# The output projection in chunks of 128 tokens, in the order of the output

## The reference

```python
# _gn: group norm, 32 groups of 12 channels, mean and variance over an image
x = x + attention(_gn(x), w_qkv, pos_emb, w_out, b_out)
# attention: shift 3 rows up and 3 columns left, windows of 7x7
qkv  = roll(x, (-3, -3)) @ w_qkv.T
dots = einsum('bhwid,bhwjd->bhwij', q, k) * 32 ** -0.5 + pos_bias + shift_mask
out  = einsum('bhwij,bhwjd->bhwid', softmax(dots), v)      # back to (B, H, W, 384)
out  = roll(out @ w_out.T + b_out, (3, 3))
```

## Time and profile before

| | us |
|---|---|
| runs | 4302.73, 4302.84, 4304.71; median 4302.84 |
| profiled execution | 4301.36 |
| its span | 4299.6 |

### The profile page before, as it was taken

How to read it: one execution, slowest core, us unless ns; L and a number is a source line. 1 busy time by engine, 2 the same in 40 slices (tenths; PEclk the granted TensorE clock), 3 DMA queues, 4 the chain that set the end, 5 groups by cost and what they waited for, 6 DMA issues and landing times.

```text
span 4299.6 us, 166334 instructions
## 1 busy us (share of the span) xinstructions
PE 4151.4 (97%) x65384; PEld 2982.5 (69%) x65384; DVE 3717.4 (86%) x9283; ACT 2271.7 (53%) x4225; POOL 2223.2 (52%) x1933
## 2 busy tenths in 40 slices
PE   3999999999999999999999999999999999999998
PEld 1677767777777767777677677777777777776776
DVE  5888888888888888888888888888888888888887
ACT  0555555555555555555555555555555555555554
POOL 1555555555555555555455555555555555555554
PEclk9999999999999999999999999999999999999999
DMA  4445444444444444444444444444534444444442
GB/s 125 102 111 126 106 112 117 110 114 112 113 118 106 115 120 103 113 125 106 112 116 112 113 113 111 120 110 108 123 101 113 125 105 112 117 111 113 102 105 62
DMA packets 231108, 479.07 MB, mean 111 GB/s; under 512 B 39009, under 2 KB 140898, under 8 KB 222818
## 3 DMA queue, kind: packets, MB, share of 16 engines
q1 hardware_dynamic: 230338, 468.43, 43.1%
HBM read 159.99 MB, written 77.07 MB: 55 GB/s over the span
## 4 chain that ended last, share of the span: by engine, by line
PE 65%; SPq 12%; DVE 10%; DMA 6%; ACT 4%; issue 4%; POOL 0%; DVEq 0%; ACTq 0%; POOLq 0%
PE ps_pj L1102 22%; PE ps_post L1198 12%; PE ps_pj L1098 9%; SPq L466 8%; DMA stack<-qk 6%; PE ps_post L1189 4%; PE ps_sa L1136 3%; PE ps_st L1166 3%; PE ps_pv L1182 3%; PE ps_pv L1181 2%; PE ps_pv L1180 2%; PE ps_st L1136 2%; ACT ph L681 2%; PE ps_pj L1086 2%; SPq L401 2%
## 5 line engine op out<-in xcount | busy, mean ns | idle before, releaser
L575 POOL TENSOR_TENSOR rb<-tq,cst 128x588 bf16<-128x588 bf16 x512 | 606.4, 1184 | 1698.7 <-ACT tq L668 1698.7
L607 ACT ACTIVATE qk<-ps_pj 128x392 f16<-128x392 f32 x768 | 381.9, 497 | 953.9 <-PE ps_pj L1102 947.8
L681 ACT ACTIVATE ph<-ps_st,sc 64x588 f16<-64x588 f32 x1024 | 772.2, 754 | 6.5
L1102 PE MATMUL ps_pj<-xh,wh 128*128 128x392 f16 x2304 | 765.9, 332 | 6.9 <-POOL xl L539 4.1
L1102 PE MATMUL ps_pj<-xh,wl 128*128 128x392 f16 x2304 | 765.0, 332 | 0.0
L1102 PE MATMUL ps_pj<-xl,wh 128*128 128x392 f16 x2304 | 764.8, 332 | 0.0
L878 DVE TENSOR_TENSOR qk<-ps_pj,qk 128x392 f16<-128x392 f32 x768 | 433.1, 564 | 383.7 <-ACT qk L607 377.6
L561 POOL TENSOR_TENSOR pl<-pf,ph 64x588 f16<-64x588 f32 x512 | 650.3, 1270 | 149.6 <-POOL rb L575 133.7
L547 POOL TENSOR_TENSOR xb<-xs,bout 98x384 f32<-98x384 f32 x512 | 513.8, 1004 | 107.9 <-DMA out<-xb 85.6
L966 DVE TENSOR_TENSOR pl<-pf,ph 64x588 f16<-64x588 f32 x512 | 529.0, 1033 | 0.1
L1180 PE MATMUL ps_pv<-vh,ph 128*128 128x33 f16 x6144 | 516.3, 177 | 1.6 <-DVE pl L966 1.6
(11 more groups left out here) (107 smaller groups left out, 8887.3 us busy)
## 6 DMA issues: line engine op xcount, KB each, us to landing
stack<-qk SPq DMA_DIRECT2D x1536, 147.0 KB
sx<-in_x SPq DMA_DIRECT2D x66, 1176.0 KB
xs<-in_x SPq DMA_DIRECT2D x384, 84.0 KB
out<-xb SPq DMA_DIRECT2D x384, 84.0 KB
xs<-in_x SPq DMA_DIRECT2D x384, 63.0 KB
out<-xb SPq DMA_DIRECT2D x384, 63.0 KB
xs<-in_x SPq DMA_DIRECT2D x128, 66.0 KB
out<-xb SPq DMA_DIRECT2D x128, 66.0 KB
```

The costliest lines, as they stand in the source:

```text
L575: nc.gpsimd.tensor_tensor(rb[:, :, :, :], tq[:, :, :].unsqueeze(2).broadcast_to([128, 2, HH, N]), const_of("own_head").unsqueeze(1).unsque ...
L681: e = nc.scalar.activation(ph[rows, :, w * PAD:w * PAD + N].rearrange("p (a h) n -> p a h n", a=2), ps_st[rows, :, 0:HH * N].rearrange("p ...
L1102: m = mm(ps_pj[bank][:, 0:RT].rearrange("p (w n) -> p w n", w=NW), wa[:, c, o:o + 128], xa[:, b, c, :, 0:N], **on)
```

## The change

The projection no longer takes the 98 tokens of a pair, but 128 tokens of a row in the order of the output. A row of 392 tokens gives three chunks of 128 and a rest of 8; the rests of 16 rows (two images) make one further chunk. `ath` and `atl` hold two whole rows, and ScalarE and VectorE write a pair's tokens into their places in the row (pair 3 in two parts, as it wraps). At p=3 ScalarE copies the rest of the last finished row to `overh` and `overl` (`keep_over`). The projection stands at the same place of a step, but at p=2, p=3 and p=0 for the chunks 0, 1 and 2 (`chunk_at`), and at p=1 only for the chunk of rests, in one row of 16. 392 projections of nine matmuls take the place of 512.

`xb` gets x by a second load from memory, directly in the order of chunks, six steps ahead (`load_chunk`); POOL adds the bias to it in place, two steps ahead. Stores are one DMA a chunk (two where an image ends within it or for the chunk of rests). The reload of `xs` no longer waits for the residual. In SP's program the stack is issued at p=1, after the store and chunk load of that step and before its reload. The new tiles take the place in memory of the raw weights.

```diff
+CHUNKS, OVER, SHARE = RT // 128, RT % 128, 128 // (RT % 128)
+XB, XB_AHEAD, BIAS_AHEAD = 8, 6, 2
+def chunk_at(t):
+    row, p = divmod(t, PAIRS)
+    row, part = {2: (row - 1, 0), 3: (row - 1, 1), 0: (row - 2, 2), 1: (row - 2, CHUNKS)}[p]
+    if not 0 <= row < ROWS or part == CHUNKS and row % SHARE != SHARE - 1:
+        return None
+    return row, part
...
+        ath = sb("ath", [128, 2, KC, RT], f16)
+        atl = sb("atl", [128, 2, KC, RT], f16)
+        overh = sb("overh", [128, KC, 128], f16)
+        overl = sb("overl", [128, KC, 128], f16)
...
+        def attended_parts(at, row, p):
+            to = at[:, row % 2, :, :].rearrange("p c (r w) -> p c r w", w=W)
+            from_ = at_out[:, :, 0:PT].rearrange("p c (r w) -> p c r w", w=2 * WS)
+            first = 2 * WS * p + DISP
+            n = min(2 * WS, W - first)
+            parts = [(to[:, :, :, first:first + n], from_[:, :, :, 0:n])]
+            if n < 2 * WS:
+                parts.append((to[:, :, :, 0:2 * WS - n], from_[:, :, :, n:2 * WS]))
+            return parts
...
-                reach(s_xb, 8 * tk.n + j + 1)
...
-                    if p == 2 and not (tk.last and odd):
-                        stack_row(1 - odd, unit_count(tk, 4 * odd + 1, "k", 2), 8 * n + 4 * odd)
...
-                    if not (tk.first and k < 3):
-                        store(t - 3, tk, k - 3)
+                    store(t)
+                    load_chunk(t + XB_AHEAD)
+                    if p == 1 and not (tk.last and odd):
+                        stack_row(1 - odd, unit_count(tk, 4 * odd + 1, "k", 2), 8 * n + 4 * odd)
...
+            def residual(t):
+                if not chunk_at(t):
+                    return
+                o = chunks_before(t)
+                pool.wait_ge(s_dense[o % XB], moved(o))
+                nc.gpsimd.tensor_tensor(xb[:, o % XB, :], xb[:, o % XB, :], bout[:, :], ALU.add).then_inc(s_xb, 1)
...
+                    if k % 4 == 3 and t > 3:
+                        keep_over(t - 4)
...
+            def keep_over(t):
+                row = t // PAIRS
+                act.wait_ge(s_al, t + 1)
+                if row >= SHARE:
+                    act.wait_ge(s_out, CHUNK_INDEX[row // SHARE * SHARE - 1, CHUNKS] + 1)
+                for over, of in ((overh, ath), (overl, atl)):
+                    ins = nc.scalar.activation(over[:, :, over_columns(row)], of[:, row % 2, :, RT - OVER:RT], ACT.Copy)
+                ins.then_inc(s_over, 1)
...
             def project_out(t):
-                pe.wait_ge(s_al, t + 1)
+                if not chunk_at(t):
+                    return
+                row, part = chunk_at(t)
+                pe.wait_ge(s_al, min(t - 2, PAIRS * ROWS))
+                need(pe, s_fin, chunks_before(t))
+                if part == CHUNKS:
+                    pe.wait_ge(s_over, row + 1)
                 for c in range(KC):
...
+                    if part == CHUNKS:
+                        high, low = overh[:, c, :], overl[:, c, :]
+                    else:
+                        high, low = (a[:, row % 2, c, part * 128:part * 128 + 128] for a in (ath, atl))
+                    for n_, (a, w) in enumerate(((high, woh), (high, wol), (low, woh))):
+                        m = mm(ps_post[:, 0:C], a, w[:, c, :], start=c == 0 and n_ == 0, stop=c == KC - 1 and n_ == 2)
```

More of the change, by code:

```diff
@@ L65, in constants @@
                 pin[place(kind, r, wc), kind, w * N + r * WS + c] = 1
[L66 to L69, removed]
+                pout[w * PAD + r * WS + c, place(0, r, wc)] = 1
+    pads = [w * PAD + i for w in range(2) for i in range(N, PAD)]
+    for n, p in enumerate(pads):
+        pout[p, PT + n] = 1
     tok = np.arange(N)
@@ L174, in ahead_image, with chunks_before, pieces, moved @@
         return self.image + (self.part + 1) // PARTS
+CHUNKS, OVER, SHARE = RT // 128, RT % 128, 128 // (RT % 128)
+IN_IMAGE = H // WS
+XB, XB_AHEAD, BIAS_AHEAD = 8, 6, 2
+STEPS = PAIRS * ROWS + 6
+def chunk_at(t):
[4 more added lines that the diff above has]
+    return row, part
+CHUNK_STEPS = [t for t in range(STEPS) if chunk_at(t)]
+CHUNK_INDEX = {chunk_at(t): o for o, t in enumerate(CHUNK_STEPS)}
+def chunks_before(t):
+    return sum(u < t for u in CHUNK_STEPS)
+def pieces(row, part):
+    if part == CHUNKS:
+        half = OVER * IN_IMAGE
+        return [(half * i, half * i + half, row // IN_IMAGE + i + 1 - SHARE // IN_IMAGE, None) for i in range(SHARE // IN_IMAGE)]
+    image, r = divmod(row, IN_IMAGE)
+    out, top, a, b = [], (WS * r + DISP) * W, part * 128, part * 128 + 128
+    cut = H * W - top
+    if a < cut:
+        out.append((0, min(b, cut) - a, image, top + a))
+    if b > cut:
+        out.append((max(a, cut) - a, 128, image, max(a, cut) - cut))
+    return out
+def moved(o):
+    return 16 * sum(len(pieces(*chunk_at(CHUNK_STEPS[i]))) for i in range(o % XB, o + 1, XB))
 def step_units(tk, k):
@@ L398, in move_row, with chunk_of, over_columns @@
             for a, b, d in pieces:
[L399 to L403, removed]
+                eng.dma_start(tile_of[a:b], d).then_inc(sems, 16)
+        x_flat, y_flat = (a.rearrange("b h w c -> b (h w) c") for a in (x, y))
+        def chunk_of(dram, image, token, n):
+            if token is None:
+                top = (WS * IN_IMAGE + DISP - 1) % H
+                return dram[image, top:H:WS, W - OVER:W, :]
+            return (x_flat if dram is x else y_flat)[image, token:token + n, :]
+        def attended_parts(at, row, p):
[7 more added lines that the diff above has]
+            return parts
+        def over_columns(row):
+            image, r = divmod(row, IN_IMAGE)
+            at = OVER * (IN_IMAGE * (image % (SHARE // IN_IMAGE)) + (r + 1) % IN_IMAGE)
+            return slice(at, at + OVER)
         def rows_of(tk, odd):
@@ L513, in _ @@
                 image(m)
[L514 to L517, removed]
+            for t in range(8 * (LAST + 1), STEPS):
+                store(t)
+                load_chunk(t + XB_AHEAD)
+            for o in range(len(CHUNK_STEPS) - XB, len(CHUNK_STEPS)):
+                sp.wait_ge(s_store[o % XB], moved(o))
         @block.gpsimd
@@ L583, in step @@
                         x_lows(tk, k)
-                    if not (tk.last and k + LEAD >= 8):
-                        residual(t + LEAD, n, k + LEAD)
+                    residual(t + BIAS_AHEAD)
             def image(m):
@@ L594, in _ @@
             split_probabilities(8 * (LAST + 1) - 1, 8 * (LAST + 1))
+            pool.wait_ge(s_pl[1], 8 * (LAST + 1))
+            for t in range(8 * (LAST + 1), STEPS):
+                residual(t + BIAS_AHEAD)
         @block.scalar
@@ L698, in _ @@
             attended_high(end - 1)
+            keep_over(end - 1)
         @block.vector
@@ L1012, in step @@
                     between(5)
-                    if not (tk.first and k < 3):
-                        output(t - 3, k - 3)
+                    output(t)
                     between(5)
@@ L1032, in _ @@
             normalize(end - 2)
-            output(end - 3, 5)
+            output(end)
             split_probabilities(end - 1)
@@ L1037, in _ @@
             normalize(end - 1)
-            output(end - 2, 6)
+            output(end + 1)
             attended_low(end - 1)
-            output(end - 1, 7)
+            for t in range(end + 2, STEPS):
+                output(t)
         @block.tensor
@@ L1219, in step @@
                         units(tk, k, 1)
-                    if not (tk.first and k < 3):
-                        project_out(t - 3)
+                    project_out(t)
                     if not (tk.last and k >= 4):
```

116 lines of the change are left out of this document (64 added, 52 removed).

## The result

| | before | changed |
|---|---|---|
| runs, us | 4302.73 to 4309.22 | 4250.67 to 4252.28 |
| median, us | 4303.77 | 4251.65 |
| ratio to before | | 0.9878, interval 0.9864 to 0.9892 |
| profiled execution / span, us | 4301.36 / 4299.6 | 4250.67 / 4248.9 |

The account below looks back on a forecast made before the run. TensorE, busy 97% of the span, was taken as the bound. Terms -29 - 7 - 17 + 4 - 1.5 + 4 = -47 us gave 4255 profiled, 4256 median; own range 4240 to 4270, wider range 4225 to 4290.

Parts of the forecast that it names:

- Projection at p=1: At p=1, k2 must wait for q2's low part, so removing 1.46 us of projection gains 0.28: 104 x 0.28 = 29 us.
- Finishing steps: p=1 steps where VectorE finishes the statistics: the output leaves its queue, 0.45 us gained in each of 15, 7 us.
- Stack: Issued one place earlier in SP's program, it starts 1.7 us earlier; 39 waits of first scores go, 17 us.
- Second load of x: 0.6 MB more to read in a row, 3.1 us of DMA time, costed at nothing.
- Rival 3: The second load of x delays the stack, so next row's first scores come 1.4 us late: 4449; chance 0.07.
- Strided writes: Runs of 14 columns make VectorE's low part 7% slower, paid at p=3: 4 us lost, bounds 0 and 59.
- Ends: Start: one dense projection gone, -1.5 us. End: four chunks behind the last pair where one stood, +4 us.
- Rival 4: A new TensorE wait of 1.2 us in each row could cost clock, 162 us: 4418; chance 0.02.

Follow-up runs that it names:

- e3: Changed kernel with nine, or six, matmuls of 384 columns put back at p=1, results unused, no output or store: nine 4279.75 us, six 4251.09 us.
- e4: Changed kernel with unit q2 moved right behind k1, ahead of the weighted values of p=1: 4163.43 us.
- e5: Changed kernel with chunk 2 projected at p=1 and the chunk of rests at p=0: 4205.0 us.
- e1: Kernel before with only the stack's place changed, issued at p=1 after that step's store and not at p=2: 4283.93 us.
- e2: Changed kernel with the stack issued at p=2 again, first thing of the step: 4254.61 us.
- e6: Changed kernel with each dense chunk of x loaded twice, the second time to a tile that nothing reads: 4249.71 us.
- e8: The e4 kernel with six matmuls added at p=1, results unused: 4252.25 us.
- e7: Kernel before with only unit q2 moved right behind k1 at p=1: 4282.19 us.

## Why the prediction was right, point by point

- *Projection at p=1*, forecast 104 x 0.28 = 29 us. The median step fell from 9.18 to 8.90, and the waits are 104. The wait's own length was forecast as 1.18 us between matmul starts, and the profile puts 1.01 us of idle time there, since x0's last matmul record ends 0.50 us behind the first one's start, where in the earlier trace rows the projection started at 0.34. e3 and e4 show the cause from both sides: work put into the wait is free, and the wait removed is time. The changed kernel has the counterproof in itself. In its last tick no x unit stands at p=1, so k2 uses the bank of k1, two units back, and not that of q2. There the step fell from 8.49 to 7.03 us, the whole 1.46, and the chain shows q2 and k2 (18 matmuls) without a gap:

```profile
4178.02 0.06 PE ps_sa L1257 x2
4178.07 3.06 PE ps_pj L1205 x18
4181.14 0.37 PE ps_st L1269 x4
```

  So the forecast's 104 steps were 102 that gained 0.28 to 0.29, this one, and one that lost: t=5, in the second row, takes 9.56 us after 9.18. There TensorE waits 0.97 us ahead of k2 and 0.50 for the shift rows, which the forecast had not looked at. Together they are 30 us. That the list also counts 104 waits is chance: they are the 102, the step t=5, and the kernel's first p=1 step, which had the wait before too.
- *Finishing steps*, 15 x 0.45 = 7 us. They fell from 11.28 to 10.87 us (the same distances), 15 x 0.41 = 6 us. That it is VectorE's lost output which gives this, as forecast, fits two runs: nine matmuls on TensorE leave these steps at 10.87 (e3), and with an output at p=1 they take 11.28 (e5).
- *Stack*, 17 us. The waits fell from 17.4 us to none. The amount is right, the reason given was half of it. I laid it to the new place in SP's program. e1 shows that the place alone does it in the kernel before; e2 shows that the changed kernel needs the new place for only 3.4 of the 17.4 us; by SP's queue the missing store of p=1 does the rest. The two overlap, and only one of them pays.
- *Second load of x*, nothing. e6: a third load is free too. Rival 3 falls.
- *Strided writes*, 7%, 4 us. VectorE's low part of a whole pair went from 456 to 472 ns, 3.5%; ScalarE's high part from 416 to 448, 8%; the copies of the rests take 212 ns, as estimated:

```profile
L1019 DVE TENSOR_TENSOR atl<-ps_post,ath 128x294 f16<-128x294 f32 x384 | 181.3, 472 | 2.7 <-ACT ath L747 1.6 <-issue 1.1
L747 ACT ACTIVATE ath<-ps_post 128x294 f16<-128x294 f32 x384 | 171.9, 448 | 10.6 <-PE ps_post L1292 2.0
...
L756 ACT ACTIVATE overh<-ath 128x24 f16<-128x24 f16 x128 | 27.2, 212 | 0.6 <-DVE atl L1019 0.6
```

  p=3, where this could have cost time, is unchanged at 7.03 us. The 4 us were not spent, so this term was too large; its lower bound, 0, was right.
- *Ends*, +4 and -1.5. The steps 3 to 5, where projections are gone, take 1.8 us less; the first step starts 0.9 us earlier, which is no more than this start differs among the other kernels here (115.0 to 117.6 us). The tail, from the start of the last full step, takes 26.7 us instead of 19.1, +7.5: the term that was mis-sized. Four projections at 2.37 us each had been counted at full clock. The last 49 us of both kernels, before first, show what the chip granted (third number from the right):

```profile
4250.00:4299.00 49.00, 34.07 (x612) 24.76 (x610) 30.87 (x63) 17.69 (x33) 15.17 (x13) 0.96 0.15 42
```

```profile
4200.00:4249.00 49.00, 33.50 (x456) 20.35 (x454) 21.78 (x46) 12.83 (x28) 17.87 (x16) 0.71 0.15 50
4232.50:4239.30 6.80, 5.92 (x18) 2.40 (x18) 0.64 (x2) 0.33 (x2) 0.00 (x0) 0.50 0.08 29
4240.20:4244.30 4.10, 3.25 (x18) 1.62 (x18) 0.62 (x1) 0.00 (x0) 0.00 (x0) 1.00 0.30 98
```

  The last row has no units of a next row, so TensorE waits often there, and with its projections put off it has less to do still. Waits of the tail and two of its projection matmuls:

```profile
4227.74 0.52 PE L1292 MATMUL ps_post<-cst,av 128*128 128x128 f32 x3 [0.80 <-DVE xb L1063]
...
4230.47 0.90 PE L1292 MATMUL ps_post<-cst,av 128*128 128x128 f32 x3 [0.92 <-DVE av L1054]
...
4232.58 0.50 PE L1310 MATMUL ps_post<-woh,ath 128*128 128x384 f16 x1 [1.21 <-DVE atl L1019]
...
4232.88 0.53 PE L1310 MATMUL ps_post<-wol,ath 128*128 128x384 f16 x1
```

  The first two of the four chunks run at a clock of 0.50, the level of 1.2 GHz, their matmuls 0.32 us apart; the last two at 1.00, 2.4 GHz, 0.16 apart. Two chunks of nine at 0.16 us more each are 2.9 us; with the forecast 4 that is 6.9 of the 7.5. The tail's clock is not steady from kernel to kernel: e2, e3 with six and e6, which end with the same work, have tails of 29.6, 27.2 and 27.1 us.
- *Rival 4, the clock in steady state.* The wait of 1.0 us in each row left the clock at 1.00 in the windows above. In e4 waits do reach it. Ahead of the shift rows of a finishing tick's step p=3 (k=7) TensorE waits 1.68 us, and the window behind has a clock of 0.51; and behind a wait of 0.92 us ahead of k2 in a finishing step the clock is 0.50:

```profile
1046.78 0.22 PE L1257 MATMUL ps_sa<-eb,mt 128*128 128x49 bf16 x2 [1.68 <-DVE mt L1045]
```

```profile
1046.80:1050.20 3.40, 3.23 (x12) 1.58 (x13) 1.83 (x5) 2.20 (x4) 2.46 (x3) 0.51 0.29 103
1791.00:1794.40 3.40, 3.40 (x15) 1.83 (x15) 2.67 (x5) 0.50 (x1) 2.40 (x2) 0.50 0.27 66
```

  The same waits do not always do it. Of the 11 waits of 1.57 to 1.69 us in e4 six were followed by a low clock, of the 14 of 1.46 to 1.70 us in e8 ten, of the 15 of 0.92 us in e4 three, and of the 104 of 0.97 to 1.01 us in the changed kernel none. What decides between them is not shown.

  The Trainium skill's rule, in "TensorE: Matmul & The Clock Gate", section "A second HAM failure mode: psum-queue depth-cycling", that short idle times between groups make the clock swing, is borne out by the last row and by some of the waits in e4 and e8, and not by one wait of a microsecond in a step of 8.9.

The sum, by the distances of all 511 steps, changed kernel less before: p=1 -36.4 us, p=0 -18.8, p=2 -2.1, p=3 +0.1 (the first 16 steps, -3.4, are in these); the first step starts 0.9 us earlier, and the tail is +7.5: -50.6, against -50.7 between the spans. The stack's waits are 17.4 of the 18.8 at p=0. The rest there, and the 2 us at p=2, nearly all in finishing ticks, were in no term of the forecast, and I have run nothing on them.

That the sum came out 4 us from the forecast, -50.6 after -47, is in part luck. The term of p=1 and that of the stack, 46 of the 47, were right in size, but the tail cost 3.5 us more than forecast, and against it stand the 4 us of strided writes that were not spent and some 3 us at p=0 and p=2 that no term had.

The expectations of the experiments erred more than the prediction, and each time on VectorE, POOL or the ticks with a finishing step (e4 by 47 us and e7 by 17 from the nearer end of the range, e5 by 15, e8 by 12).

## What to carry to other kernels

Work that is removed from a full engine is worth only what is left after the next wait behind it: look at what the removed work stood in front of, and when that one's semaphore would be met without it. An early iteration in which the work is missing anyway (here the first p=1 step) shows the new wait in the trace of the old kernel. Once the wait is known, the order of the work behind it is the next edit, and can be worth more than the change itself (88 us for one line of the table here against 52).

## What the runs showed of the hardware

SP's issues here take less time for a dense chunk than for a pair's rows: 0.35 us for a chunk, and 0.74 to 0.78 for a part of a pair (1.48 for two), in the changed kernel:

```profile
1984.30 1.48 SPq L449 DMA_DIRECT2D xs<-in_x  x2
1985.88 0.36 SPq L577 DMA_DIRECT2D xb<-in_x  x1
...
1993.27 8.79 SPq L536 DMA_DIRECT2D stack<-qk  x12
```

The prediction had counted 0.74 us for each of 28 issues a row. Waits far shorter than the 3.42 us of the prologue can be followed by a low clock: some of 1.5 to 1.7 us in e4 and e8 and some of 0.92 us in e4 were (six of 11, ten of 14, three of 15), and so was a series of 0.8 to 1.2 us in the last row of the changed kernel (mean clock 0.71 over 49 us). A single wait of 1.0 us a row, in the changed kernel, left it at 1.00 from 120 to 4190 us. So the length of one wait does not decide it alone.
